# An attention and mixture-of-experts kernel: stack loads, statistics and narrow values in another order, and the last batch's scatters without landing waits

## The chip, the core and the metric

The kernel runs as one program on one core of a Trainium2 chip. Five engines work from their own instruction streams and wait for each other through semaphores: PE (TensorE, matrix products and transposes), DVE (VectorE), ACT (ScalarE), POOL (GpSimd) and SP (SyncE, which here only issues DMAs). The metric is the device time of one execution in microseconds, lower is better.

## What is computed

Two layers, each an attention block and a mixture of experts with the same expert weights, on x of 4 x 1024 x 256 in float32:

```python
x = x + attn_a(layernorm(x), ...)   # 16 heads of 16, causal, softmax with distance decay
x = x + ffn(layernorm(x), ...)
x = x + attn_b(layernorm(x), ...)   # 16 heads of 16, causal, plain softmax
x = x + ffn(layernorm(x), ...)

def ffn(x):                         # 4096 tokens
    shared = sum(relu(x @ w1 + b1) @ w2 + b2 for 2 shared experts) / 2
    probs = softmax(x @ router_w + router_b)       # 32 experts
    gates = top 6 of probs, divided by their sum
    routed = sum(gates[:, e] * (relu(x @ w1[e] + b1[e]) @ w2[e] + b2[e]) for 32 experts)
    return shared + routed
```

## The kernel before

Both layers run the same code, in four phases with a barrier of all five engines behind each (`phase_end`, L371). x lies in SBUF as 32 tiles of 128 tokens in four quarters of 8 tiles. A quarter is a batch, a block is half of one (512 tokens), so there are 8 blocks, numbered 0 to 7.

**Start of a layer.** DVE takes mean and variance of a quarter (`input_var`, L746, with ACT's square root, L1226), scales (`input_scales`) and normalises blocks (`normalise_block`, L733). In layer 1 it first adds the two expert sums into x: quarters 0 and 1 on DVE (L1209), 2 and 3 on POOL (L1506), all in the order of their loads. After the last layer the same adds stand before the result's stores.

**Phase 0, projections.** For each block TensorE forms q, k and v with split float32r products (L1541) and transposes v (L1551). DVE and POOL split q and k into a high and a low part (L782, L1414: POOL's `qk_lo`), DVE copies v into a staging tile `vst` with 32 columns a head: 16 values, then ones. SP stores q, k and v in HBM scratch (`store_block`, L412). Attention reads them back in units of four heads of one batch, 16 units. A unit's q and k lie in a stack, one of three slots. A slot is first zeroed (slot 0: half by DVE, L806, half by POOL, L1423, after all q and k work of block 5), then gets constant rows (`load_rows`, L434), then q and k (`load_stack`, L440), then, after a wait for the constant rows, two more rows (L443). The slots share their space with x's transposed blocks 0 to 3. Before the barrier TensorE and DVE compute unit 0's row maxima (L1576, L817). SP then waits for all stores (L472) and loads the negated maxima as a row of the stack (`load_neg_max`, L478), which the first scores need.

**Phase 1, attention.** Per unit 12 steps of scores (L1590), exponentials (ACT, L1282) and value products (L1607), with the next unit's maximum jobs and the routing of the batch before woven in. The value product's weights are 32 columns of `vreg`; a column of ones gives the softmax sum. Routing of a batch ends with `place_rows`, which computes the row index of each of a token's six copies. POOL's `dispatch(b)` (L1446) then scatters the batch's rows into per-expert lists: 48 indirect DMAs of 128 rows of 1280 B, six for each tile. They are counted on six semaphores, three for each half of the batch. In batches 0 and 1 POOL waits ahead of each third scatter for the three before, in batches 2 and 3 ahead of each for the one three places earlier. `dispatch(3)` falls into phase 2.

**Phase 2, shared experts.** TensorE computes them for the 8 blocks while batch 3 is routed; SP loads the remaining routed weights, the last of them (`load_w1(17, 32)`, L499) after the last shared sum is stored. The phase ends for SP when all scatters have landed.

**Phase 3, routed experts.** 128 tiles of 256 rows; POOL adds the results into the two sums (L1491).

On SP the weights for phases 2 and 3 that fit early are loaded at the end of phase 1: w1 of experts 10 to 16 in the last unit's turn, then the shared weights and w2 of 16 to 23 and 27 to 31, then the first two blocks of x for the shared experts.

## Time and profile before

| | |
|---|---|
| runs shown | 3131.27, 3128.80, 3125.81 us (median 3128.8) |
| the profiled execution | 3135.21 us, its span 3133.4 us |
| PE busy | 2614.6 us, 83% |
| DVE busy | 2075.2 us, 66% |
| ACT busy | 1643.9 us, 52% |
| POOL busy | 1395.5 us, 45% |
| DMA | 494.55 MB, mean 158 GB/s |
| mean granted clock of TensorE | 0.928 of 2.4 GHz |

The span runs from the first to the last instruction; the execution's own time is 1.8 us more. Busy shares are means over four kinds of phases that have different limits, so a change in one phase is read from that phase's rows: who is idle, until what. A timeline row gives start, duration, engine, line, operation, destination and source; in brackets stands the idle time before it and what ended it.

### The profile page before, as it was taken

Reading aid. Unit: us, or ns where it says so; the run is one execution under the profiler, and the core shown is the slowest. Engines: PE = TensorE matmul, PEld = TensorE weight load, DVE = VectorE, ACT = ScalarE, POOL = GpSimd, SP = SyncE. Lnnn points to the kernel's source line nnn. Section 1 sums busy time; section 2 is a strip of 40 time slices with the busy share of each in tenths; the row PEclk is TensorE's granted clock in tenths of the full one; section 3 lists DMA queues with packets and bytes.
Section 4 is the critical chain, followed back from the end, with each engine's and each line's share of the span. In section 5 each row is a group of like instructions: output and inputs, shape, how many; then the busy total and the mean of one; then the engine's idle time right before and its main releaser. Section 6 shows DMA issues by size and latency. Waiting matters only on the chain.

```text
span 3133.4 us, 72452 instructions
## 1 busy us (share of the span) xinstructions
PE 2614.6 (83%) x17832; PEld 1946.6 (62%) x17832; DVE 2075.2 (66%) x4624; ACT 1643.9 (52%) x2861; POOL 1395.5 (45%) x1046
## 2 busy tenths in 40 slices
PE   7699999999973799999385999999998728999992
PEld 5455565555553788888363555655555618888882
DVE  8666676776561687777395666766765517777872
ACT  3245444444411788888331554434444208888882
POOL 3430002314245688888544200023142457888885
PEclk9899999999987999999787999999999869999996
DMA  6975645555665789889859644564557648898988
GB/s 222 230 162 128 144 100 108 143 123 164 198 227 192 137 151 157 153 153 155 175 172 221 137 84 89 100 134 128 121 161 223 231 164 149 153 155 154 155 155 204
DMA packets 317281, 494.55 MB, mean 158 GB/s; under 512 B 55706, under 2 KB 225052, under 8 KB 311772
## 3 DMA queue, kind: packets, MB, share of 16 engines
q1 hardware_dynamic: 224908, 361.85, 43.9%
q0 software_dynamic: 92160, 130.08, 25.1%
q8 instruction: 106, 1.74, 0.2%
q14 instruction: 107, 0.88, 0.1%
HBM read 264.26 MB, written 256.77 MB: 166 GB/s over the span
## 4 chain that ended last, share of the span: by engine, by line
PE 45%; DMA 18%; issue 17%; POOL 6%; DVE 6%; SPq 3%; DVEq 2%; POOLq 1%; ACT 1%; ACTq 1%
PE ps L1576 10%; DMA expert_rows<-x 9%; PE ps L1590 9%; PE ps L1607 8%; DMA expert_sum<-x,route_u 5%; PE ps L1859 5%; PE ps L1877 4%; POOL expert_rows L1464 3%; PE ps L1594 2%; PE ps L1580 2%; SPq L424 2%; POOL expert_sum L1491 1%; DMA split<-rows_scratch 1%; DVE split L1171 1%; POOL split L1414 1%
## 5 line engine op out<-in xcount | busy, mean ns | idle before, releaser
L1282 ACT ACTIVATE work<-ps 128x1024 f32<-128x1024 f32 (+3 forms) x768 | 594.9, 810 | 679.0 <-PE ps L1594 458.1
L1464 POOL DMA_INDIRECT expert_rows<-x x372 | 365.4, 982 | 1272.1 <-DVE x L979 805.6
L1491 POOL DMA_INDIRECT expert_sum<-x,route_u x512 | 825.7, 1613 | 195.7 <-issue 92.5
L817 DVE TENSOR_REDUCE small<-ps 128x1 f32<-128x512 f32 (+3 forms) x1216 | 727.3, 656 | 216.9 <-PE ps L1580 145.1
L1576 PE MATMUL ps<-split 128*128 128x512 f32 (+3 forms) x1536 | 510.6, 408 | 72.3 <-DVE work L845 32.2
L1590 PE MATMUL ps<-split 128*128 128x512 f32 (+3 forms) x1536 | 501.6, 406 | 28.1 <-DMA split<-split 27.0
L1859 PE MATMUL ps<-split 128*88 128x256 f32 x3072 | 417.0, 285 | 86.2 <-DVE split L1171 50.4
L1859 PEld LDWEIGHTS ps<-split 128*88 128x88 f32 x3072 | 362.9, 155 | 134.9 <-issue 132.9
L1576 PEld LDWEIGHTS ps<-split 128*128 128x128 f32 x1536 | 275.0, 199 | 269.7 <-DVE small L817 144.8
L1877 PE MATMUL ps<-split 97*128 97x256 f32 x3072 | 408.8, 282 | 2.4 <-DVE split L1186 2.2
L1877 PEld LDWEIGHTS ps<-split 97*128 97x128 f32 x3072 | 384.7, 189 | 3.0 <-issue 2.9
L1590 PEld LDWEIGHTS ps<-split 128*128 128x128 f32 x1536 | 300.8, 202 | 86.7 <-ACT work L1282 40.8
L1607 PE MATMUL ps<-work,split 128*32 128x512 f32 (+3 forms) x3072 | 330.5, 505 | 2.8 <-ACT work L1282 2.8
L1346 ACT ACTIVATE x<-ps,osb 88x256 f32<-88x256 f32 x512 | 232.1, 471 | 30.8 <-issue 15.9
L1847 PE MATMUL ps<-ident,x 128*128 128x128 f32 x1024 | 156.7, 276 | 105.7 <-DMA osb<-in_b1r 105.7
L1360 ACT ACTIVATE split<-split 97x512 fp32r x256 | 161.4, 631 | 151.6 <-issue 138.3
L1594 PE MATMUL ps<-maskk,identb 128*128 128x128 bf16 x1024 | 234.6, 236 | 0.0
L1155 DVE CAST split<-work 128x352 fp32r x256 | 102.8, 402 | 188.7 <-issue 145.2
L1372 ACT ACTIVATE x<-ps,osb 128x256 f32<-128x256 f32 x512 | 212.1, 465 | 18.6 <-DMA expert_sum<-x,route_u 10.9
L1179 DVE TENSOR_TENSOR split<-split 97x512 fp32r<-97x512 f32 x256 | 176.3, 689 | 16.3 <-issue 7.4
L1847 PEld LDWEIGHTS ps<-ident,x 128*128 128x128 f32 x1024 | 120.3, 143 | 107.0 <-issue 107.0
L1580 PE MATMUL ps<-maskq,identb 128*128 128x128 bf16 (+2 forms) x704 | 185.7, 264 | 0.0
(179 smaller groups left out, 3152.2 us busy)
## 6 DMA issues: line engine op xcount, KB each, us to landing
x<-expert_rows SPq DMA_DIRECT2D x256, 320.0 KB
split<-qks_scratch SPq DMA_DIRECT2D x192, 256.0 KB
qks_scratch<-split SPq DMA_DIRECT2D x64, 512.0 KB, 4.5
expert_rows<-in_pads SPq DMA_DIRECT2D x65, 320.0 KB, 16.0
v_scratch<-work SPq DMA_DIRECT2D x64, 256.0 KB, 4.3
split<-v_scratch SPq DMA_DIRECT2D x32, 512.0 KB, 14.3
xT_scratch<-split SPq DMA_DIRECT2D x16, 1024.0 KB
split<-xT_scratch SPq DMA_DIRECT2D x16, 1024.0 KB
```

The costliest lines, as they stand in the source:

```text
L817: v.tensor_reduce(cols[:, heads[0]:heads[0] + len(heads), i], ps[:, task_bank(n), 0:w * len(heads)].rearrange("p (h k) -> p h k", k=w), AX ...
L1282: c.activation(pexp[:, (s % 2) * 2 + h, :, BLK - w:], ps[:, 2 * h:2 * h + 2, BLK - w:], ACT.Exp).then_inc(s_pe, 1)
L1464: pool.indirect_dma_start(rows, bass.IndirectOffsetOnAxis(ap=posu[b][:, t * 8 + k:t * 8 + k + 1], axis=0), row_tile(b, t // TPB, t % TPB), ...
L1491: pool.indirect_dma_start(acc[r], bass.IndirectOffsetOnAxis(ap=idx[:, j, k:k + 1], axis=0), ye[:, r3, k, :], None, compute_op=ALU.add).the ...
L1576: last = mm(bank[:, e, :], stack[:, r, 0, h, i * P:i * P + P], stack[:, r, 1, h, first:first + w], start=e == 0, stop=not diagonal and e = ...
L1580: last = mm(bank[:, :, w - P:w], identb[:, :], maskq[:, :].unsqueeze(1).broadcast_to([P, len(heads), P]), start=False, stop=True, skip_gro ...
L1590: last = mm(ps[:, h, BLK - w:], stack[:, r, 1, h, kb * P:kb * P + P], stack[:, r, 0, h, (qt + 1) * BLK - w:(qt + 1) * BLK], start=True, st ...
L1594: last = mm(ps[:, h, BLK - w:BLK - w + P], identb[:, :], maskk[:, :], start=False, stop=True, skip_group_check=True)
L1607: last = mm(ps[32 * h:32 * h + 32, 6, BLK - w:], vreg[:, r, kb, h, :], pexp[:, (s % 2) * 2 + h // 2, h % 2, BLK - w:], start=kb == 0, stop ...
L1847: last = tr(ps[:, r, k * TT + n * P:k * TT + n * P + P], xrow[:, r3, n, k * P:k * P + P], ident[:, :])
L1859: last = mm(ps[0:HC, 2 + c, 0:TT], w1e[:, r, ws, k * HID + c * HC:k * HID + c * HC + HC], xe[:, r, xp, k * TT:k * TT + TT], start=e == 0 a ...
L1877: last = mm(ps[:, 4 + 2 * (j % 2) + n, 0:D], he[0:HB, r, xp, c * TT + n * P:c * TT + n * P + P], w2e[0:HB, r3, ws, c * D:c * D + D], start ...
```

## The change

The change has five parts.

1. Values without padding: a head takes 17 columns (16 values, one column of ones) instead of 32, in `vst`, in the scratch and in `vreg`. The value product still reads 32 columns, at a step of 17, so that 15 of them belong to the next head and their results are not used. `vst` is laid out by unit, so that DVE copies four quarters of heads instead of two halves.
2. Slot 0 is zeroed by POOL alone, around block 4's low parts. Its constant rows are issued ahead of block 4's stores, its q and k ahead of block 5's. SP issues the stores of blocks 5, 6 and 7 in a row, then slot 1. The wait for all stores moves behind the load of the maxima row.
3. The early weights move forward: w1 of 10 to 16 into the turn of unit 13, the shared weights and w2 into that of unit 14.
4. The statistics, scales and first two normalised blocks of quarter 0 move to the end of the layer before, between DVE's two adds (`first_quarter`). For layer 0 they stand ahead of the loop, and they also run once after the last layer.
5. `dispatch(3)` has no waits between its scatters. The wait ahead of its first one stays. Batch 2 keeps its waits.

```diff
-    vds = nc.dram_tensor("v_scratch", (NU, P, NQB, HG * 32), F32, kind="Internal").ap()
+    vds = nc.dram_tensor("v_scratch", (NU, P, 2, TPB * HG * VW), F32, kind="Internal").ap()
...
-                with sp.Fori(0, B - 1) as b:
+                with sp.Fori(0, B - 2) as b:
                     for r in range(2):
                         store_block(b, r)
...
                 load_rows(0)
                 for r in range(2):
                     sp.wait_ge(s_pd[r], (L * B + 1) * 64 + 64)
+                store_block(B - 2, 0)
                 load_stack(0, 0)
-                store_block(B - 1, 0)
+                store_block(B - 2, 1)
+                for r in range(2):
+                    store_block(B - 1, r)
                 load_rows(1)
                 load_stack(1, 1)
-                store_block(B - 1, 1)
                 phase_end(sp, L, 0)
...
-                for r in range(2):
-                    sp.wait_ge(s_pd[r], (L * B + B) * 64 + 64)
-                    sp.wait_ge(s_vd[r], (L * B + B) * 64 + 64)
...
                 load_neg_max(0)
+                for r in range(2):
+                    sp.wait_ge(s_pd[r], (L * B + B) * 64 + 64)
+                    sp.wait_ge(s_vd[r], (L * B + B) * 64 + 64)
                 load_values(0, 0)
...
                 for u in range(NU):
+                    if u == NU - 2:
+                        sp.wait_ge(s_pv, (L * NU + NU - 3) * NS + NS + 2)
+                        if L == 0:
+                            sp.wait_ge(s_init, 128)
+                        apart(sp)
+                        sp.dma_start(raw.rearrange("p r n -> p (r n)"), wsd).then_inc(s_raw, 16)
+                        load_w2(16, 24)
+                        load_w2(27, 32)
...
-                    if u == NU - 1:
+                    if u == NU - 3:
                         sp.wait_ge(s_mr, TASKS + route_task(B - 2, 3) + 1 + 3)
                         apart(sp)
                         load_w1(EARLY, 17)
-                sp.wait_ge(s_pv, (L * NU + NU - 3) * NS + NS + 2)
-                apart(sp)
-                sp.dma_start(raw.rearrange("p r n -> p (r n)"), wsd).then_inc(s_raw, 16)
                 sp.dma_start(b1, a["b1"]).then_inc(s_shared, 16)
-                load_w2(16, 24)
-                load_w2(27, 32)
...
+            def first_quarter(N):
+                input_var(N, 0)
+                input_scales(N, 0)
+                for r in range(2):
+                    normalise_block(N, r, r)
...
-                    for f in range(2):
-                        last = v.tensor_copy(vst[:, r, :, 8 * f:8 * f + 8, 0:HD],
-                                             ps[:, 6 + f, :].rearrange("p (t h c) -> p t h c", t=TPB, h=8))
+                    for u in range(HG):
+                        last = v.tensor_copy(vst[:, r, u, :, :, 0:HD],
+                                             ps[:, 6 + u // 2, :].rearrange("p (t h c) -> p t h c", t=TPB, h=8)
+                                             [:, :, u % 2 * HG:u % 2 * HG + HG, :])
...
-                dve.wait_ge(s_pj, (L * NBLK + 4) * 6)
-                v.memset(stack32[64:P, 0, 0], 0.0).then_inc(s_zq, 1)
...
                     v.tensor_tensor(xq, xq, summ[:, q], ALU.add).then_inc(s_ca[q], 1)
+                    if q == 0:
+                        first_quarter(L + 1)
...
-                with pool.Fori(0, B - 1) as b:
+                with pool.Fori(0, B - 2) as b:
                     for r in range(2):
                         qk_lo(b, r)
                 pool.wait_ge(s_pj, (L * NBLK + 4) * 6)
-                pool.wait_ge(s_pl, (L * NBLK + 6) * 4 + 4)
-                apart(pool)
-                p.memset(stack32[64:P, 0, 1], 0.0).then_inc(s_zero[0], 1)
-                pool.wait_ge(s_zero[0], L + 1)
+                for r in range(2):
+                    pool.wait_ge(s_pl, (L * NBLK + 4 + r) * 4 + 4)
+                    apart(pool)
+                    p.memset(stack32[64:P, 0, r], 0.0).then_inc(s_zero[0], 1)
+                    pool.wait_ge(s_zero[0], L * 2 + r + 1)
+                    apart(pool)
+                    qk_lo(B - 2, r)
...
-                            if n >= AHEAD and b >= B - 2:
+                            if n >= AHEAD and b == B - 2:
...
-                            elif n >= AHEAD and n % AHEAD == 0:
+                            elif n >= AHEAD and n % AHEAD == 0 and b < B - 2:
...
-                        last = mm(ps[32 * h:32 * h + 32, 6, BLK - w:], vreg[:, r, kb, h, :],
+                        at = (kb * HG + h) * VW
+                        last = mm(ps[32 * h:32 * h + 32, 6, BLK - w:], vreg[:, r, at:at + 32],
```

Three places where instructions move. First the SP queue at the end of phase 0; its destinations and sources are `split<-rows_scratch` for constant rows, `split<-qks_scratch` for q and k, `split<-split` for the maxima row. Before, from the end of the loop over blocks 0 to 5 on:

```order
L434 DMA split<-rows_scratch 20x4x1024 [waits first_query_stack_zeroed,stack_zeroed0,constant_rows_stored]
L440 DMA split<-qks_scratch 16x4x1024 [waits qk_stored1,qk_stored0]
L440 DMA split<-qks_scratch 16x4x1024 x5
L443 DMA split<-rows_scratch 2x4x1024 [waits constant_rows_loaded0]
L418 DMA qks_scratch<-split 128x2x512 [waits qk_lo_done]
L424 DMA v_scratch<-work 128x4x128 [waits v_staged]
L434 DMA split<-rows_scratch 20x4x1024 [waits stack_zeroed1]
L440 DMA split<-qks_scratch 16x4x1024 x6
L443 DMA split<-rows_scratch 2x4x1024 [waits constant_rows_loaded1]
L478 DMA split<-split 1x32x128 [waits phase_done,v_stored1,qk_stored1,task_done,v_stored0,qk_stored0]
```

And now, from the end of the loop over blocks 0 to 3 on:

```order
L434 DMA split<-rows_scratch 20x4x1024 [waits stack_zeroed0,constant_rows_stored]
L420 DMA qks_scratch<-split 128x2x512 [waits qk_lo_done,qk_stored0,qk_stored1]
L426 DMA v_scratch<-work 128x272 [waits v_staged]
L440 DMA split<-qks_scratch 16x4x1024 x6
L443 DMA split<-rows_scratch 2x4x1024 [waits constant_rows_loaded0]
L420 DMA qks_scratch<-split 128x2x512 [waits qk_lo_done]
L434 DMA split<-rows_scratch 20x4x1024 [waits stack_zeroed1]
L440 DMA split<-qks_scratch 16x4x1024 x6
L443 DMA split<-rows_scratch 2x4x1024 [waits constant_rows_loaded1]
L477 DMA split<-split 1x32x128 [waits phase_done,task_done]
```

Slot 0 has moved ahead of two blocks' stores, slot 1 behind the last one, and the maxima row no longer waits for stores.

Then POOL from its last wait for row indices on, which is `dispatch(3)`. Before, its head, of which the last two rows stand for 45 such waits:

```order
L1450 REGISTER_ALU [waits row_indices_ready]
L1464 DMA expert_rows<-x 140288x320 [waits rows_dispatched12,rows_dispatched10,rows_dispatched11]
L1464 DMA expert_rows<-x 140288x320 x2
L1457 ISA
L1464 DMA expert_rows<-x 140288x320 [waits rows_dispatched00]
L1464 DMA expert_rows<-x 140288x320 [waits rows_dispatched01]
```

And now, to its end:

```order
L1462 REGISTER_ALU [waits row_indices_ready]
L1476 DMA expert_rows<-x 140288x320 [waits rows_dispatched12,rows_dispatched10,rows_dispatched11]
L1476 DMA expert_rows<-x 140288x320 x41
L1476 DMA expert_rows<-work,x 140288x320 x6
L377 REGISTER_ALU
```

47 of the 48 scatters now stand in a row; 45 had a wait of their own.

Last, DVE at the end of a layer. Before, behind the barrier of phase 3:

```order
L1207 REGISTER_ALU [waits phase_done]
L1209 TENSOR_TENSOR x<-x,split 128x2048 [waits sums_loaded0]
L1209 TENSOR_TENSOR x<-x,split 128x2048 [waits sums_loaded1]
L698 REGISTER_ALU
L698 COMPARE_AND_BRANCH
```

And now, with the steps of the variance left out:

```order
L1215 TENSOR_TENSOR x<-x,split 128x2048 [waits sums_loaded0]
L733 REGISTER_ALU [waits x_loaded0]
L687 BN_STATS small<-x 128x6 [waits sums_added0]
L687 BN_STATS small<-x 128x6 x7
L727 TENSOR_SCALAR work<-x,osb 128x256 [waits dve_chain,xT_psum_ready]
L1215 TENSOR_TENSOR x<-x,split 128x2048 [waits sums_loaded1]
L760 REGISTER_ALU
L760 COMPARE_AND_BRANCH
```

The statistics and the normalising of two blocks stand between the two adds, ahead of the loop's branch.

## Rows read from the trace of the kernel before

**Rows 1.** Timeline of the SP queue: start, duration, instruction, count [idle before, by whom ended].
```profile
100.02 1.45 SPq L434 DMA_DIRECT2D split<-rows_scratch  x2
...
127.49 2.14 SPq L434 DMA_DIRECT2D split<-rows_scratch  x2
...
140.85 0.24 SPq L443 DMA_DIRECT2D split<-rows_scratch  x1
...
159.18 1.22 SPq L478 DMA_DIRECT2D split<-split  x2
```

**Rows 2.** Timeline of PE, 62 to 168 us.
```profile
124.29 1.11 PE L1576 MATMUL ps<-split 128*128 128x128 f32 x4 [14.00 <-DMA split<-rows_scratch]
...
162.09 0.79 PE L1590 MATMUL ps<-split 128*128 128x512 f32 x1 [13.52 <-DMA split<-split]
```

**Rows 3.** Windows, phase 0: stretch, length, busy by engine, PEclk, DMA share, GB/s.
```profile
84.00:102.00 18.00, 17.15 (x87) 14.06 (x87) 15.12 (x16) 8.26 (x12) 13.64 (x9) 1.00 1.01 338
105.00:117.00 12.00, 4.43 (x23) 3.30 (x21) 3.08 (x4) 2.14 (x4) 10.86 (x5) 0.77 1.04 117
153.00:157.00 4.00, 0.00 (x0) 0.00 (x0) 0.00 (x0) 1.28 (x1) 0.84 (x1) 0.50 0.83 262
```

**Rows 4.** Timeline of POOL, phase 0: block 4's low parts, slot 0's memset.
```profile
76.47 5.95 POOL L1414 TENSOR_TENSOR split<-work,split 128x512 fp32r<-128x512 f32 x4 [5.03 <-DVE split L782]
...
90.98 3.52 POOL L1423 MEMSET split<- 64x4096 f32 x1 [0.16 <-POOL split L1414]
```

**Rows 5.** Timeline of POOL, scatters of batches 2 and 3, layer 0.
```profile
830.81 0.96 POOL L1464 DMA_INDIRECT expert_rows<-x  x1 [41.66 <-DVE x L979]
...
840.37 0.96 POOL L1464 DMA_INDIRECT expert_rows<-x  x1 [4.84 <-DMA expert_rows<-x]
...
933.10 0.96 POOL L1464 DMA_INDIRECT expert_rows<-x  x1 [8.57 <-DMA expert_rows<-x]
...
1010.48 0.96 POOL L1464 DMA_INDIRECT expert_rows<-work,x  x1 [0.30 <-DMA expert_rows<-work,x]
1011.75 0.96 POOL L1464 DMA_INDIRECT expert_rows<-work,x  x1 [0.31 <-issue]
```

**Rows 6.** Windows, the ends of phase 2 in layers 0 and 1.
```profile
990.00:999.00 9.00, 0.00 (x0) 0.00 (x0) 0.00 (x0) 0.00 (x0) 2.88 (x3) 0.50 1.05 388
...
2548.00:2568.00 20.00, 0.00 (x0) 0.00 (x0) 0.00 (x0) 0.00 (x0) 15.12 (x17) 0.50 0.34 123
```

**Rows 7.** Timeline of the SP queue, layer 0: the last routed weights.
```profile
988.44 0.71 SPq L499 DMA_DIRECT2D work<-in_w1r  x1
```

**Rows 8.** Timeline of PE, layer 0: the first tile's transposes.
```profile
1026.11 1.09 PE L1847 MATMUL ps<-ident,x 128*128 128x128 f32 x4 [44.23 <-DMA osb<-in_b1r]
```

**Rows 9.** Timeline of POOL, layer 1: first and last scatter of batch 3.
```profile
2490.36 0.97 POOL L1464 DMA_INDIRECT expert_rows<-x  x1 [2.41 <-DMA expert_rows<-x]
...
2570.32 0.97 POOL L1464 DMA_INDIRECT expert_rows<-work,x  x1 [0.30 <-issue]
```

**Rows 10.** Timeline of DVE, layer 0: batch 3's rows are placed.
```profile
914.60 0.15 DVE L979 COPY work<-x 128x1 f32<-128x1 f32 x1
```

**Rows 11.** Timelines of DVE at the start of layer 0 and of layer 1.
```profile
8.96 2.71 DVE L684 BATCH_NORM_STATS2 small<-x 128x6 f32<-128x256 f32 x8 [0.18 <-issue]
...
16.86 0.95 DVE L764 CAST split<-work 128x1536 fp32r<-128x1536 f32 x1
...
1548.89 2.29 DVE L1209 TENSOR_TENSOR x<-x,split 128x2048 f32<-128x2048 f32 x1 [29.87 <-DMA split<-expert_sum]
...
1564.42 2.71 DVE L684 BATCH_NORM_STATS2 small<-x 128x6 f32<-128x256 f32 x8 [4.35 <-issue]
...
1577.33 0.95 DVE L764 CAST split<-work 128x1536 fp32r<-128x1536 f32 x1
```

**Rows 12.** Timeline of DVE at the kernel's end.
```profile
3104.26 2.29 DVE L1209 TENSOR_TENSOR x<-x,split 128x2048 f32<-128x2048 f32 x1 [28.62 <-DMA split<-expert_sum]
```

**Rows 13.** Line L1607, its weight loads: duration ns min/median/max, first and last start.
```profile
L1607 PEld LDWEIGHTS ps<-work,split x3072: 106/109/156, 170.5 to 2400.3; 128*32 128x32 f32 x192
```

More of the change, by code:

```diff
@@ L674, in _ @@
             dve.sem_inc(s_thl, 2)
-            chain = [0]
+            chain, layer = [0], [0]
             def link(ins):
@@ L686, in statistics, with linked, row_var @@
                 return last
+            def linked():
+                dve.wait_ge(s_chain, layer[0] * CHAIN + chain[0])
+            def row_var(st, sv):
+                me, ve, mo, vo = (st[:, :, s] for s in (1, 2, 4, 5))
+                v.tensor_tensor(sv[:, 0], me, mo, ALU.subtract)
+                v.tensor_tensor(sv[:, 1], me, mo, ALU.add)
+                link(v.tensor_tensor(sv[:, 2], ve, vo, ALU.add))
+                linked()
+                v.tensor_tensor(sv[:, 3], sv[:, 0], sv[:, 0], ALU.mult)
+                link(v.tensor_scalar(sv[:, 4], sv[:, 2], 1.0 / D, EPS, ALU.mult, ALU.add))
+                linked()
+                v.scalar_tensor_tensor(sv[:, 5], sv[:, 3], 0.25, sv[:, 4], ALU.mult, ALU.add).then_inc(s_var, 1)
@@ new lines, in normalise_block, with input_var @@
+            def normalise_block(N, blk, r):
+                dve.wait_ge(s_tp, N * NBLK + blk + 1)
+                for j in range(TPB):
+                    t = blk * TPB + j
+                    last = v.tensor_scalar(xn[:, r, j, :], x[:, ds(t * D, D)], sv[:, 8, ds(t, 1)],
+                                           sv[:, 9, ds(t, 1)], ALU.mult, ALU.add)
+                last.then_inc(s_xn, 1)
+            def input_var(N, q):
+                dve.wait_ge(s_x[q], 16)
+                dve.wait_ge(s_ca[q], N + 1)
+                apart(dve)
+                link(statistics(8 * q, 8))
+                linked()
+                row_var(stat[:, 8 * q:8 * q + 8, :], sv[:, :, 8 * q:8 * q + 8])
```

111 lines of the change are left out of this document (41 added, 70 removed).

## The prediction

> **What bounds the kernel now.** I read the page's shares and its chain of waits first: TensorE is the busiest engine and carries most of the chain, DMA comes next. TensorE's part lies in attention and in the tile loop, which the change leaves alone. The DMA part lies in three gaps where TensorE is idle, once per layer or between layers, and there the stage timelines decide.
>
> Gap one is the end of phase 0. TensorE has no work for 14.00 us until the first stack has landed at 124.29, and again 13.52 us until the row of negated maxima arrives at 162.09 [rows 2]. The SP queue issues the constant rows for slot 0 at 100.02, those of slot 1 at 127.49, and the maxima row only at 159.18 [rows 1]. DMA is saturated there: share 1.01 at 338 GB/s over 84 to 102, and also 1.04 at only 117 GB/s while rows and stacks are written [rows 3]. So the gap is a queue of bytes, and an order within it.
>
> Gap two is the end of phase 2. The last 96 scatters (batches 2 and 3) run on POOL from 830.81 to 1012.71; batch 3 alone from 933.10, 48 scatters in 79.6 us [rows 5]. TensorE idles 44.23 us until the first tile's transpose at 1026.11, 13.4 us after POOL's last issue [rows 8]. The last weights were issued at 988.44 [rows 7]. In layer 1 batch 3 takes from 2490.36 to 2571.29, 80.9 us [rows 9].
>
> Gap three is between the layers: the first quarter is summed by 1551.18, but its statistics start at 1564.42 [rows 11].
>
> **The end of phase 0, with thinner v stores.** Sizes are from the shapes. A block stores q and k with 4 x 512 KB, 2.1 MB, and v with 4 x 256 KB, 1.05 MB. At 338 GB/s the first takes 6.2 us; the v stores alone run at 262 GB/s [rows 3], 4.0 us. The new v is 17 of 32 columns, 0.56 MB; in pieces of 1088 B instead of 512 B I take the 338 GB/s, 1.6 us. A block falls from 10.2 to 7.8 us. Rows plus stack of one slot are 0.66 + 1.57 = 2.2 MB at 117 GB/s, 19 us (5.6 and 13.4).
>
> As a check, the old kernel from 84 on has four blocks and two slots, 41 + 38 = 79 us, so it would end at 163; its maxima row left at 159.18, so the model is 4 us too long. Now the new order. POOL finishes block 4's subtractions at 82.42 [rows 4]; one memset (3.52 us, as the one at 90.98 [rows 4]) stands before that, the second behind it, so the rows of slot 0 are issued at 86, not 100. Then rows 5.6, block 4 7.8, stack 13.4: slot 0 lands at 113 instead of 124.3. The maximum jobs take 24.3 us (from 124.29 to where TensorE goes idle, 13.52 us ahead of 162.09 [rows 2]) and then end at 137. But behind the stack wait three block stores (23 us) and slot 1 (19 us), the DMA ends at 86 + 31 + 38 = 155, less the 4 us of the check 151. The maxima row leaves when SP is through its last row wait, and is then behind slot 1's stack in the queue: first scores at about 153 instead of 162.09. **Gain 9 us a layer, 18 together.** Bounds: 5, if the v stores stay at 262 GB/s and nothing else overlaps; 16, if a small DMA isn't held up by the stack, since then only SP's wait counts (rows of slot 1 issued at 131, 11 us to land as from 127.49 to 140.85 [rows 1], then 2.9 us as now).
>
> That a small load waits here shows in the 2-partition load behind slot 0's stack: its landing ends TensorE's 14.00 us, long after its issue. The Trainium skill, "DMA: Bandwidth & Descriptors", section "Queues, rings and completion order", says that on each DMA engine descriptors are consumed in ring order; by that rule the 16 us bound is out and 9 stands, without it the sum would be 14 us larger. It speaks against the full worth of the reordering, since SP now issues more ahead of the maxima row.
>
> **The scatters.** Without waits POOL issues one each 1.27 us (1010.48 to 1011.75 [rows 5]; the many other unheld neighbours read alike), so 48 take 47 x 1.267 + 0.96 = 60.5 us. Against 79.6 and 80.9 us that takes off 19.1 and 20.4. The DMA can take that: over 2548 to 2568, with scatters alone at about this pace, the share is 0.34 [rows 6]. The wait ahead of batch 3 for batch 2's second half stays. Batch 2 gains too: its first and fourth scatter are 9.56 us apart [rows 5], at free pace 3.8. The transfers that crowd them are the shared weights, the w2 parts and w1 (4.9 MB), which now go out one to two units earlier. So batch 3 starts 5.8 earlier; at least 0, at most 18, as its rows are placed at 914.75 [rows 10].
>
> Next in line in layer 0 is w1: 2.7 MB issued at 988.44, DMA full over 990 to 999 at 388 GB/s [rows 6, 7], landed about 1001, with the first tile's rows right behind. So the first transpose comes near 1004 instead of 1026.11: 22 us, though POOL is done 24.9 earlier. In layer 1 w1 has landed before 2548, since DMA then moves scatters alone [rows 6], 23 us before POOL ends, so POOL's 5.8 + 20.4 = 26.2 us count nearly in full. **Gain 48.** Bounds: 39.5 - 3 without batch 2's part and with stores slowed by the denser scatters; 61 with batch 3 starting at its earliest in layer 1 and layer 0 held at 23.
>
> **The moved loads.** Raw shared weights, w2 and w1, 4.9 MB at 338 GB/s, are 15 us at the border of units 13 and 14. They pass the maxima row of unit 15 on SP, which is due two thirds into a unit of 42 us ((830.81 - 162.09) / 16). Cost 0; if that cover were gone, up to 15 us a layer. The scatters of batch 1 are queued beside them, but their successor starts at 830.81 after 41.66 us of idle POOL [rows 5].
>
> **Between the layers.** The first quarter's statistics to normalised rows take 7.9 us undisturbed (8.96 to 16.86 at the kernel's start [rows 11]). From 1551.2 they end at 1559.1, the second add (2.29) at 1561.4; the 4.35 us behind it that the row at 1564.42 shows make it 1565.8, where the weight split can start; before, it started at 1577.33 [rows 11]. That is 11.5 us, of which POOL's two adds may eat what they now cost DVE: 1564.42 to 1577.33 is 12.9 us for the 7.9. **Gain 7**, bounds 4 and 11. At the very end the same block sits before the second add: the first ends at 3106.55 [rows 12], then 7.9 and 2.29 give 3116.7, 4 us later than the second add's end now. The stores leave in order, and the last one waits for POOL's second add (L1506), which nothing moves: **cost 1**, bounds 0 and 5.
>
> **Small edits at 0**: the v memset shrinks 16 times, DVE loses one memset at slot 0, the v copies become four halves instead of two; TensorE is the busier engine there. Together -2 to +2 us.
>
> Sum: 18 + 48 + 7 - 1 = 72. The profiled execution, 3135.2 us (span 3133.4), would become 3063. The median of the runs, 3128.8, is 6.4 lower; from it, 3057.
>
> **Rivals.**
> 1. The maxima row isn't held up by slot 1's stack: 16 a layer instead of 9, 3043. For it: the stacks are written by many short transfers in parallel. Against: the 14.00 us above. 20%.
> 2. The scatter queue fills and holds POOL instead of the semaphores. POOL waited up to 8.57 us for a landing [rows 5], six or seven scatters' worth at free pace; what the queue holds beyond three shows nowhere. Then only batch 2's part is left of the 48, some 12: 3093. Against: the share of 0.34. 12%.
> 3. Slower: the weights of the value products are now 32 columns at a step of 17, 68 B, so they start unaligned and overlap. TensorE loads them 3072 times, in 0.109 us each (median [rows 13]). If a load grew by 23 ns and nothing hid it, all 72 us were gone; at twice 0.109 with half hidden it is +167 - 72 = +95, 3224. Against: each load can run under the product of the head before, and moves as many bytes as now. 3%.
> 4. The new order does nothing, since slot 0 is still late, and the layer start is eaten by POOL: only the scatters' 48, 3081. 8%.
>
> **How the numbers follow.** Forecast 57%: 3057. Its own bounds: gains of 10 + 36 + 4 - 5 - 2 = 43 to 32 + 61 + 11 + 2 = 106, so 3086 to 3023; both ends need every bound at once. 3028 to 3088 holds most of the forecast, rivals 1 and 4: about 82%. A measurement can tell 0.2%, 6 us. Faster 0.96, same 0.01, slower 0.03.
>
> **What would show it.** Right: slot 0's rows issued near 86, maximum jobs from about 113, first scores near 153; batch 3's scatters 1.27 us apart with no landing waits; first tile transposes 22 and 26 us nearer to the start of batch 2; weight split 7 us or more sooner after 1551.2. Wrong: scatters of batch 3 with gaps or long issues, w1 landing later than 1001, value-weight loads above 0.109 us, or a wait for the maxima row in units 14 and 15.

## The result, and the profile after

The changed kernel is slower: 3218.4 us in the median of 4 runs (3193.6 to 3223.9), against 3127.7 (3125.8 to 3131.3) for the kernel before on the same chip. The ratio is 1.0273, with a 95% interval of 1.0217 to 1.0329. Forecast were 3057 us, with 3028 to 3088 as the range; the result lies 161 us above it, and on the other side of the kernel before. The profiled run took 3213.5 us, its span is 3211.7 at a mean clock of 0.916 (before: 3133.4 at 0.928), so 78.3 us are to be found in the trace.

First where they are. Each boundary of a stage has a row that stands right behind it. Of the kernel after, from SyncE's timeline (start us, us, engine and line, operation, out<-in): the load of the first unit's maxima, which opens phase 1, the table's load, which opens phase 2, and the first tile's rows, which open phase 3, for both layers:

```profile
150.22 1.23 SPq L477 DMA_DIRECT2D split<-split  x2
887.01 0.33 SPq L581 DMA_DIRECT2D work<-in_table  x1
1062.87 0.36 SPq L641 DMA_DIRECT2D x<-expert_rows  x1
...
1746.85 1.25 SPq L477 DMA_DIRECT2D split<-split  x2
2477.53 0.33 SPq L581 DMA_DIRECT2D work<-in_table  x1
2654.70 0.37 SPq L641 DMA_DIRECT2D x<-expert_rows  x1
```

The same of the kernel before (its first is in [rows 1]):

```profile
842.06 0.33 SPq L578 DMA_DIRECT2D work<-in_table  x1
1022.98 0.38 SPq L638 DMA_DIRECT2D x<-expert_rows  x1
...
1719.26 1.25 SPq L478 DMA_DIRECT2D split<-split  x2
2403.15 0.33 SPq L578 DMA_DIRECT2D work<-in_table  x1
2581.49 0.37 SPq L638 DMA_DIRECT2D x<-expert_rows  x1
```

And VectorE's timeline of after, at the first sum of each layer (before: [rows 11] and [rows 12]); the statistics of the next layer's first quarter now follow it:

```profile
1593.49 2.29 DVE L1215 TENSOR_TENSOR x<-x,split 128x2048 f32<-128x2048 f32 x1 [30.81 <-DMA split<-expert_sum]
...
3182.60 2.29 DVE L1215 TENSOR_TENSOR x<-x,split 128x2048 f32<-128x2048 f32 x1 [29.02 <-DMA split<-expert_sum]
3185.04 2.71 DVE L687 BATCH_NORM_STATS2 small<-x 128x6 f32<-128x256 f32 x8
```

The differences between these rows give the ledger:

| stretch, us | before | after | change |
|---|---|---|---|
| start to maxima of unit 0, layer 0 | 159.2 | 150.2 | -9.0 |
| phase 1, layer 0 | 682.9 | 736.8 | +53.9 |
| phase 2, layer 0 | 180.9 | 175.9 | -5.1 |
| phase 3, layer 0 | 525.9 | 530.6 | +4.7 |
| first sum to maxima of unit 0, layer 1 | 170.4 | 153.4 | -17.0 |
| phase 1, layer 1 | 683.9 | 730.7 | +46.8 |
| phase 2, layer 1 | 178.3 | 177.2 | -1.2 |
| phase 3, layer 1 | 522.8 | 527.9 | +5.1 |
| first final sum to the end | 29.1 | 29.1 | 0.0 |

100.7 of the loss are in phase 1, of which the forecast said nothing at all, and phase 2 has not given the 48 that it was to give.

Now the place in phase 1. Its last 45 us are nearly empty. The windows of after, 845 to 870 us (columns as in [rows 3]: busy time and instruction count of TensorE, of its weight loads, of VectorE, ScalarE and POOL, then the granted clock, the DMA engines' share, GB/s):

```profile
845.00:870.00 25.00, 0.00 (x0) 0.00 (x0) 0.00 (x0) 0.00 (x0) 18.90 (x21) 0.50 0.35 127
```

Three engines stand still, and the DMA engines are a third busy. Only POOL works, and SyncE issues nothing between 804.83 and 887.01. What each engine did there, from the timelines of PE, ScalarE, VectorE and POOL in turn (in brackets the idle time before, and what ended it):

```profile
842.52 0.66 PE L1620 MATMUL ps<-work,split 128*32 128x128 f32 x8 [6.36 <-ACT work L1290]
875.13 1.11 PE L1630 MATMUL ps<-ident,osb 128*128 128x128 f32 x4 [31.95 <-ACT osb L1278]
```

```profile
842.09 0.38 ACT L1290 ACTIVATE work<-ps 128x256 f32<-128x256 f32 x1 [3.84 <-remote]
874.40 0.60 ACT L1278 ACTIVATE osb<-ps 128x512 f32<-128x512 f32 x1 [31.93 <-remote]
```

```profile
885.53 0.26 DVE L848 RECIPROCAL small<-ps 128x16 f32<-128x16 f32 x1 [59.47 <-remote]
885.82 0.42 DVE L851 TENSOR_TENSOR work<-ps,small 128x256 f32<-128x256 f32 x1
```

```profile
822.12 0.96 POOL L1476 DMA_INDIRECT expert_rows<-x  x1 [32.92 <-issue]
...
843.03 0.96 POOL L1476 DMA_INDIRECT expert_rows<-x  x1 [0.30 <-DMA expert_rows<-x]
...
882.28 0.96 POOL L1476 DMA_INDIRECT expert_rows<-x  x1 [0.31 <-issue]
```

The last value products of unit 15 end at 843.18 (842.52 and 0.66). ScalarE's copy at L1278 (`evacuate`) waits for nothing but `s_pv`, which counts the value products, and `s_mj`, which counts TensorE's transposes and other small jobs. Both are raised by TensorE alone. Yet it starts at 874.40, 31 us after the products. TensorE's transposes at L1630 follow it within 0.13 us (875.00 to 875.13), so ScalarE's signal came at once. They end at 876.24; VectorE, which waits for them alone, starts at 885.53, 9.3 us late.
Meanwhile POOL issues batch 2's 48 scatters in 60.2 us from the first to the last, one every 1.27, where the kernel before took 92.8. Its waits for landings are still in the code and hardly hold it: its idle time between two of them is 0.30 us, and at most 0.69. Nothing else moves then, and the scatters land in time. That is the second half of the finding. The moved loads (a w2 stretch, the raw weights, w1) used to fill the DMA engines at just this time; the windows 815 to 820 us, of before and then of after:

```profile
815.00:820.00 5.00, 5.00 (x31) 2.21 (x31) 0.55 (x3) 2.53 (x5) 0.00 (x0) 0.70 1.03 370
```

```profile
815.00:820.00 5.00, 4.68 (x33) 2.13 (x34) 3.50 (x16) 3.87 (x5) 0.00 (x0) 1.00 0.00 0
```

The DMA share goes from 1.03 to 0.00, and batch 2's row forms in the gap.

Phase 2 repeats it with batch 3, whose waits the change did remove. POOL's first and last scatter and TensorE's timeline of after:

```profile
954.58 1.20 POOL L1476 DMA_INDIRECT expert_rows<-x  x1 [71.34 <-DVE work L985]
...
1015.56 0.96 POOL L1476 DMA_INDIRECT expert_rows<-work,x  x1 [0.30 <-issue]
```

```profile
1023.17 1.09 PE L1805 MATMUL ps<-ident,work 128*128 128x128 f32 x4 [28.28 <-DVE work L1110]
...
1054.71 0.63 PE L1805 MATMUL ps<-ident,work 128*128 128x128 f32 x4 [0.87 <-DVE work L1110]
1071.44 2.00 PE L1860 MATMUL ps<-ident,x 128*128 128x128 f32 x8 [16.11 <-DMA osb<-in_b1r]
```

The 48 take 61.9 us to the end of the last, against 60.5 forecast. But they start at 954.58, where the forecast had 927: their rows are placed later, since phase 1 ends 45 us later. And phase 2's products, which ended at 981.9 in the kernel before (1026.11 less the 44.23 of waiting in [rows 8]), now end at 1055.3: the engines end phase 2, and no longer the scatters.

### The profile page after: what moved, and what is told of

Read it like the earlier page. It is cut to its first block, busy times and chain, and to the rows that moved or that the text cites. A ratio compares the mean times of both kernels' runs of the same rounds, so it can differ in the third digit from the quotient of the medians.

```text
span 3211.7 us, 72334 instructions
## 1 busy us (share of the span) xinstructions
PE 2636.3 (82%) x17832; PEld 1961.2 (61%) x17832; DVE 2082.4 (65%) x4682; ACT 1646.2 (51%) x2863; POOL 1402.4 (44%) x1048
## 4 chain that ended last, share of the span: by engine, by line
PE 47%; issue 13%; DVE 12%; DMA 12%; another core or an unknown queue 5%; POOL 3%; DVEq 2%; ACT 2%; SPq 1%; POOLq 1%; PEldq 1%; ACTq 1%; PEld 0%
PE ps L1588 10%; PE ps L1602 10%; PE ps L1620 8%; DMA expert_sum<-x,route_u 6%; PE ps L1872 4%; PE ps L1890 3%; DMA expert_rows<-x 2%; PE ps L1606 2%; PE ps L1592 2%; POOL expert_sum L1503 2%; PE ps L1665 2%; DVE split L1177 2%; PE ps L1782 1%; PE ps L1793 1%
## 5 line engine op out<-in xcount | busy, mean ns | idle before, releaser
L1588 PE MATMUL ps<-split 128*128 128x512 f32 (+3 forms) x1536 | 512.4, 409 | 65.2 <-DVE work L851 34.5
L1185 DVE TENSOR_TENSOR split<-split 97x512 fp32r<-97x512 f32 x256 | 176.2, 688 | 15.9 <-issue 8.2
L1192 DVE TENSOR_TENSOR split<-x,split 88x512 fp32r<-88x512 f32 x256 | 174.1, 680 | 13.4 <-ACT split L1359 11.7
(178 smaller groups left out, 3143.1 us busy)
```

The costliest lines, as they stand in the source:

```text
L1588: last = mm(bank[:, e, :], stack[:, r, 0, h, i * P:i * P + P], stack[:, r, 1, h, first:first + w], start=e == 0, stop=not diagonal and e = ...
```

## The experiments

All times are medians, all ratios against the kernel before on the same chip. The experiments ran on four chips, where the kernel before took 3123.9 to 3127.2 us, so differences of a few us between them mean little. **Theory A**: a long row of scatters without a pause, one every 1.27 us, makes TensorE's signals late; batch 2's row exists because of the moved loads, batch 3's because of the removed waits. **Theory B**: only the scatters without waits do harm. **Theory C**: the loads in their new place collide with the attention units. **Theory D**: it is a matter of how many scatters and bytes are under way, whatever their spacing.

### One part undone, and one part alone

`undo_issue`, the fifth part undone:

```
-                            if n >= AHEAD and b == B - 2:
+                            if n >= AHEAD and b >= B - 2:
...
-                            elif n >= AHEAD and n % AHEAD == 0 and b < B - 2:
+                            elif n >= AHEAD and n % AHEAD == 0:
```

> The changed kernel with the fifth part undone: batch 3's scatters wait for landings again. Theory A (a long row of scatters every 1.27 us makes TensorE's signals late; batch 2's row comes from the moved loads, which left the DMA engines idle from 806 to 830): the end of phase 1 still loses about 45 us a layer, because batch 2's scatters do not change (822 to 882, 60 us for 48); batch 3's may keep a pitch of 1.27 too where nothing else moves, and so the time stays above 3180, 3190 to 3230. Theory B (only the unthrottled scatters of batch 3 do harm): the loss goes, and the time is that of before less the gains of the border and of phase 0, 3085 to 3110. Theory C (the early loads collide with the attention units' own): still slow, 3200 to 3220, but with batch 2's scatters slower than 60 us.

3098.8 us (3091.3 to 3109.1), ratio 0.9909 (0.9879 to 0.9939). This is theory B's number, and theory A's lowest, 3180, was 81 us too high. The trace shows why, in ScalarE's and SyncE's timelines of this run:

```profile
830.73 0.60 ACT L1278 ACTIVATE osb<-ps 128x512 f32<-128x512 f32 x1 [4.73 <-remote]
```

```profile
833.65 0.33 SPq L581 DMA_DIRECT2D work<-in_table  x1
```

The same copy waits for the same late signal, 4.7 us instead of 31.9. Phase 1 has then ended by 833.65, SyncE's loads of phase 2 start, the scatters have to wait for landings again, and the row ends at twelve. A reading that fits is that a row is a trap that holds itself: late signals keep SyncE from issuing, and an idle DMA system keeps the row unbroken. Batch 2's code is the same in both kernels, and here it began at 817.1, in after at 822.1. Why the trap closes in the changed kernel and not here is not shown: five runs of this one lie between 3091 and 3109, four of that one between 3194 and 3224, so it isn't chance from run to run. The moved loads alone are thus not enough for the row.

`undo_loads`, the third part undone (the diff's hunks on w1, the raw weights and w2 taken back):

> The changed kernel with the third part undone: w1, the raw shared weights and w2 are loaded at the end of phase 1 again. Theory A: batch 2's scatters are held back by those loads as before (about 93 us for 48, none over 10 in a row), the 32 us wait of ScalarE for a matmul's signal at the end of phase 1 goes, about 90 us are regained; batch 3's 48 in a row still make TensorE's signals late in phase 2, so that of the 48 us forecast little is left: 3090 to 3130. Theory B: no change, 3210 to 3225, since the loss is put down to batch 3. Theory C: 3060 to 3130.

3129.9 us (3119.4 to 3143.1), 1.0014 (0.9993 to 1.0034). Theory A fits, theory B falls: 89 us come back although batch 3's scatters stay without waits. Their row still costs; TensorE's timeline in this run:

```profile
985.18 2.93 PE L1792 MATMUL ps<-split 128*128 128x512 f32 x6 [32.49 <-ACT work L1321]
```

`loads_alone`, the kernel before with the third part only:

> The kernel before with the third part alone. Theory A: batch 2's scatters run in one row of 60 us, the end of phase 1 loses 40 to 50 us a layer, 3190 to 3225. Theory B: the forecast's price for the moved loads, nothing, 3120 to 3135. Theory C: 3190 to 3225 too, but with the loss in units 13 to 15 (760 to 810), ahead of batch 2's scatters.

3142.6 us in the median of ten runs, but these spread from 3113.4 to 3207.7. The ratio, 1.002 (0.998 to 1.006), is of the seven shortest; the medians of all give 1.005. Theory A's range, from 3190 up, holds one run of the ten, and no theory named a spread. It is what the trap would make, closed in one layer, in both or in none, but the profiled run took 3120.3 and has no long row in batch 2. The runs that would show it were not profiled, so the trap is not shown here; this run shows only that the cost is not constant.

`issue_alone`, the kernel before with the fifth part only:

> The kernel before with the fifth part alone. The forecast's step: 44 to 48 us faster, 3080 to 3085. Theory A: batch 3's 48 scatters stand in one row of 61 us, in which TensorE's signals come late and phase 2's last blocks stand still, so most of the gain is lost again: 3110 to 3140. Theory B: slower than before by 40 us a layer, 3190 to 3220.

3154.3 us (3152.5 to 3160.2), 1.0082 (1.0055 to 1.0109): slower by 28, where the forecast's step says 48 faster, and 14 above theory A's range, 36 under theory B's. TensorE's timeline has one long wait in batch 3's row:

```profile
999.23 1.22 PE L1780 MATMUL ps<-split 128*128 128x512 f32 x2 [38.37 <-ACT work L1314]
```

### The length of a row

If a pause is what lets the signals through, the rows can be cut. These four start from the changed kernel, whose loads stay moved. Rows of k wait, at every k-th scatter of batches 2 and 3, for the landing of the ones before; `rows3`, `rows6` and `rows12` have k = 3, 6 and 12:

```
-                            if n >= AHEAD and b == B - 2:
-                                r, m = divmod(n - AHEAD, TPB * TOPK)
-                                pool.wait_ge(s_disp[r][m % AHEAD], ...)
-                                apart(pool)
-                            elif n >= AHEAD and n % AHEAD == 0 and b < B - 2:
+                            if n >= AHEAD and n % (AHEAD if b < B - 2 else k) == 0:
```

> The changed kernel with batches 2 and 3 issued three at a time, each three after the landing of the three before, as batches 0 and 1 are. Theory A (TensorE's signals come late in proportion to the length of a row of scatters without a pause): no row over 3, no wait of ScalarE on TensorE's signals over 5 us at the end of phase 1 or in phase 2; batches 2 and 3 take 90 to 110 us each, so that the scatters again end the layer: 3085 to 3125. Theory D (a jam by the count of scatters or their bytes, wherever the pauses are): 3150 to 3220.

> As that with rows of six in batches 2 and 3. Theory A: about 75 to 80 us a batch (48 scatters of 1.27 us and seven waits for a landing of 2.3 us), signals late by 2 us at most, 3060 to 3095, faster than rows of three. Theory D: 3150 to 3220.

> As that with rows of twelve. Theory A: some 70 us a batch, signals late by up to about 5 us near a row's end (4.3 us after nine scatters in the run without the fifth part), 3055 to 3110; with rows as short as this the jam of 32 us does not come. Theory D: 3150 to 3220.

`rows3` took 3188.8 us (3182.2 to 3200.1), 1.0206 (1.0168 to 1.0245). `rows6` took 3096.4 (3095.8 to 3102.9), 0.9909 (0.9879 to 0.9940), and `rows12` 3094.1 (3081.1 to 3107.6), 0.9891 (0.9844 to 0.9939). By the time alone `rows3` speaks for theory D (3150 to 3220), the other two against it. TensorE's waits (us in total, times, longest; 780 to 1080 us) speak against it in all three. `rows3`:

```profile
PE ps L1856 <- DMA osb<-in_b1r: 100.8, 2, 98.7
...
PE ps L1626 <- ACT osb L1278: 1.8, 1, 1.8
```

`rows6`:

```profile
PE ps L1856 <- DMA osb<-in_b1r: 51.2, 2, 49.0
...
PE ps L1801 <- DVE work L1110: 2.8, 2, 1.9
```

`rows12`:

```profile
PE ps L1856 <- DMA osb<-in_b1r: 15.9, 1, 15.9
...
PE ps L1801 <- DVE work L1110: 10.8, 3, 5.0
PE ps L1616 <- ACT work L1290: 6.9, 1, 6.9
```

In rows of three no signal is late by more than 2 us, and TensorE waits 98.7 us at the start of phase 3 for scatters that are simply too slow: 123.2 us for batch 2 and 93.9 for batch 3. Theory A's price for `rows3`, 3085 to 3125, took the pace from batches 0 and 1 too kindly. In rows of six 49.0 of that wait are left, in rows of twelve 15.9. These 15.9 are no longer due to the scatters: the changed kernel has 16.1 there, though its row ended 39 us before TensorE's last products of phase 2. Meanwhile the late signals grow to 5.0 and 6.9. The two costs trade, and the best row is in between or a mixture.

`pause` keeps the change's waits and puts POOL work between any two scatters:

```
+        idle = sb("idle", [P, 384], F32)
...
+                            if b >= B - 2:
+                                p.memset(idle[:, 0:384], 0.0)
+                                pool.drain()
                             pool.indirect_dma_start(
```

> The changed kernel with its waits as they are and a short piece of POOL work, a memset of 128 x 384 and a drain, ahead of every scatter of batches 2 and 3, so that no two stand 1.27 us apart. Theory A in its strict form (the pitch of 1.27 us is what makes the signals late, and any pause between scatters lets them through): no wait over 5 us, and the time goes by the pitch that comes out, 3090 to 3160 at 1.8 to 2.2 us. If only the landing of all issued scatters clears it, the signals stay late in the long rows of batch 3, and the time is 3180 to 3230.

3460.3 us (3458.1 to 3462.8), 1.107 (1.104 to 1.110). The pause came out far longer than meant, 3.3 us from scatter to scatter and more in batch 2, so the time is above every forecast. It does say that without dense issue no signal is late: TensorE's longest wait on VectorE's copies at L1111, which hang on them, is 1.8 us, and of TensorE's 86 updates beside batch 2 in layer 0 none is over 0.04 us late. (Batch 3 tests nothing here: TensorE is done with phase 2 before it starts.) But at 3.3 us from one to the next nearly every scatter has landed before the next is issued, so it does not tell the dense issue from the missing landings. Batch 2's row in the changed kernel does: its waits allow three scatters under way at most, and the signals are as late there as in batch 3, which has none.

`b2_rows12` changes batch 2 alone, to rows of twelve; batch 3 stays without waits:

```
+                            if n >= AHEAD and b < B - 1 and n % (AHEAD if b < B - 2 else 12) == 0:
```

> The changed kernel with one edit: batch 2's scatters in rows of twelve instead of one wait per scatter; batch 3's stay without waits, and the loads stay moved. Theory A (the price of the moved loads is batch 2's unbroken row and nothing else): the 32 us wait at the end of phase 1 goes in both layers and 80 to 90 us with it, down to the run without the third part, 3115 to 3140; the wait of about 30 us in batch 3's row of 48 stays. If the loads' place itself costs, 3180 to 3220.

3141.4 us (3121.8 to 3152.2), 1.0045 (1.0017 to 1.0072): 77 of the changed kernel's us come back, with the loads in their new place. This rules theory C out. TensorE's longest wait is now in phase 2, in batch 3's row:

```profile
PE ps L1789 <- ACT work L1322: 37.8, 1, 37.8
```

`mix_6_12` has rows of six in batch 2 and rows of twelve in batch 3:

```
+                            if n >= AHEAD and n % {B - 2: 6, B - 1: 12}.get(b, AHEAD) == 0:
```

> Batch 2 in rows of six and batch 3 in rows of twelve. In rows of six phase 2's products are done at 961 and phase 3 waits for the scatters until 1006; in rows of twelve the products are done at 998, with the scatters at 989. Theory A: batch 2 ends at 912 and batch 3 starts at 915 as in rows of six, takes 68 us as in rows of twelve and ends at 983, the products by 985: phase 3 about 10 us a layer earlier than either, 3070 to 3085. If batch 3's rows of twelve alone hold the products up: 3090 to 3100, no gain.

**3071.0 us** (3067.2 to 3082.2), 0.9833 (0.9787 to 0.9879), faster than both kernels: 53 us under before, 1.7%, with all five parts of the change in place but for the form of the waits. Its waits of TensorE:

```profile
PE ps L1856 <- DMA osb<-in_b1r: 28.2, 2, 25.9
...
PE ps L1801 <- DVE work L1110: 5.2, 4, 2.1
...
PE ps L1789 <- ACT work L1322: 4.2, 1, 4.2
```

`mix_6_24`, the same with 24 for 12, asks for the size in between:

> Batch 2 in rows of six and batch 3 in two rows of twenty-four. Theory A, now asked for the size: batch 3 takes 64 us instead of 70 and would end phase 2 by 5 us a layer earlier, but in a row of 24 (30 us) a signal of TensorE can be late by 10 to 20 us where one of twelve made it 5: 3080 to 3115, slower than 3071. If lateness is not a matter of the row's length but of rows without any end (48): 3055 to 3075.

3121.3 us (3096.7 to 3133.8), 0.9976 (0.9951 to 1.0002): 50 us slower than with twelve, a little beyond the range. The waits:

```profile
PE ps L1801 <- DVE work L1110: 19.4, 3, 18.1
...
PE ps L1789 <- ACT work L1322: 14.2, 3, 10.3
PE ps L1778 <- ACT work L1311: 6.5, 1, 6.5
```

So the longest wait behind a signal of TensorE in batch 3, layer 0, was 1.9 us in rows of six, 4.2 and 5.0 in rows of twelve (`mix_6_12`, `rows12`), 18.1 in rows of twenty-four, and 28 to 38 in the four runs with a row of forty-eight. In layer 1 it was 13 us with twenty-four and 9 to 35 with forty-eight, so the size varies from place to place. The recorded updates show the same without the detour over waits. How late at least TensorE's latest one was behind the end of its matmul, from the first scatter of a batch to 8 us behind the last, over both layers:

| scatters in a row | batches | latest update of TensorE, us |
|---|---|---|
| 1 | `pause`, batch 2 | 0.04 to 0.19 |
| 3 | `rows3`, batch 2 | 1.0 to 1.3 |
| 6 | `rows6`, both; `mix_6_12` and `mix_6_24`, batch 2 | 1.1 to 3.2 |
| 12 | `rows12`, both; `b2_rows12`, batch 2; `mix_6_12`, batch 3 | 4.4 to 7.3 |
| 24 | `mix_6_24`, batch 3 | 18.9 to 19.1 |
| 48 | after, both; `undo_loads`, `issue_alone`, `b2_rows12`, batch 3 | 13.6 to 46.8 |

In all of these stretches no update of VectorE or ScalarE was more than 0.02 us behind. (Only semaphores that one engine alone raises are counted.) Theory A's form, late in proportion to the row, holds roughly; a wait per scatter that lets a long row form is no better than none.

### The other parts, and the loads again

`parts124` is the changed kernel without its third and fifth parts, `border` the kernel before with the fourth alone:

> The changed kernel without its third and fifth parts: v's compact copy, slot 0's early zeroing and stack, and the statistics between the layers. By the forecast's terms 18 for phase 0 and 7 for the border less 1: 24 under before, 3100 to 3105. By the first trace, whose phases 0 are 4.0 and 11.9 us shorter and whose phases 3 are 4.4 and 5.0 longer: 3115 to 3120.

> The kernel before with the fourth part alone, the first quarter's statistics between VectorE's two last sums. By the forecast's terms 6 faster (7 at the border, 1 lost at the end): 3119 to 3122. If what is moved only lengthens phase 3's end by what it saves in phase 0: 3125 to 3128.

`parts124` took 3101.2 us (3092.4 to 3112.4), 0.9930 (0.9904 to 0.9955), and `border` 3113.1 (3105.5 to 3120.8), 0.9963 (0.9945 to 0.9981). The forecast's 3100 to 3105 for the first holds. The second gained 11 where 6 were forecast, and the first two parts together are left with 12 or less (10 by the ratios) instead of 18.

`mix_loads_back` takes the third part out of `mix_6_12`, and `rows_alone` is the kernel before with nothing but the rows of six and twelve:

> The run with rows of six and twelve, with the third part undone. It asks what the moved loads are worth once no long row can form. The forecast's term is nothing: 3065 to 3080. If the loads at the end of phase 1 hold batch 2's scatters back (92 us for 48 in the run without the third part, 86 to 90 with it) and meet phase 2's own loads: 3075 to 3095.

> The kernel before with nothing but batch 2's scatters in rows of six and batch 3's in rows of twelve. Theory A: of the scatters' 48 us the part that rows of twelve allow, batch 3 in 70 instead of 79 us and no long row: 10 to 15 us a layer, 3095 to 3110. If the gain needs the moved loads: 3115 to 3130.

`mix_loads_back` took 3100.0 us (3093.5 to 3107.9), 0.9898 (0.9868 to 0.9927), `rows_alone` 3115.3 (3106.5 to 3124.8), 0.9945 (0.9919 to 0.9972). The first is beyond both of its ranges, the second in the one for a gain that needs the moved loads. With the rows cut, the moved loads are worth 29 us by the medians, 20 by the ratios: batch 2's scatters take 86 to 90 us instead of 101, and batch 3 starts that much earlier. Neither half has the gain by itself. Over `parts124`, whose scatters wait as before, the cut rows bring 1 us without the moved loads (3101.2 to 3100.0), and the moved loads bring 2 without the cut rows (3098.8, `undo_issue`); both together bring 30. By the ratios these are 10, 7 and 30, so the two single gains lie within the noise, and the surplus of the pair is 13 to 27.

The changed kernel's own two steps, in one table:

| with the first, second and fourth parts, us | loads as before | loads moved |
|---|---|---|
| a wait per scatter | 3101.2 | 3098.8 |
| batch 3 without waits | 3129.9 | 3218.4 |
| rows of six and twelve | 3100.0 | 3071.0 |

## Why the prediction was wrong, step by step

- **Phase 0, 9 us a layer: its mechanism failed, and that the ledger has 9.0 in layer 0 is in part luck.** By the runs the first two parts are worth 10 to 12 for both layers, not 18. Slot 0's constant rows are issued at 88.55, where 86 was forecast. But the max jobs did not start at 113: they start at 124.84, before at 124.29 [rows 2], now held by VectorE's copies of v for the last block. (The bound of 16 also reads 11 us between two rows that are 13.4 apart; with that it is 15.) What was saved lies behind them: the stores stand ahead of the second stack, and their landings are waited for only after the maxima's load. First scores start at 155.42, not at 153; before, 162.09 [rows 2].
- **Between the layers, 7 us, less 1 at the end: right, and low if anything.** Border and phase 0 of layer 1 together were to give 16, and the ledger has 17.0; alone the part gave 11 over both. The end of the kernel costs nothing in the ledger: 29.1 us from the first final sum, before and after.
- **Compact v and its unaligned weights: right.** The value products took 508 ns each, before 505, their weight loads 0.109 us in the median, as before. The rival that put the slower outcome there, 3224 at 3%, hit the number and had the wrong mechanism. Its number is no support for it.
- **Moved loads, 0: the first step that failed.** Alone among the terms it was priced by what the loads themselves need. The prediction asked what hides them. It even saw that they had crowded batch 2's scatters, and booked the relief as a gain of 5.8 us. They were the traffic that made these scatters pause. With them gone and batch 3 without waits, the row of 48 formed, in both layers, and phase 1 became 53.9 and 46.8 us longer. With a wait per scatter in both batches the 0 was right, as a size (3101.2 to 3098.8); beside batch 3 without waits it is 89 us (3129.9 to 3218.4), and next to cut rows the same move is worth 20 to 29 in favour. So the sum failed as a sum too: it added two terms that depend on each other. Why batch 3's waits decide over batch 2's row is open.
- **Scatters without waits, 48: the second that failed.** Pace and length came as forecast, 61.9 us for 48 against 60.5. That the engines' own work in phase 2 would keep its pace beside them was taken for granted, and that step is false: the row makes TensorE wait 28 to 38 us in one place, and the step that was to gain 48 costs 28 by itself (29 beside the first, second and fourth parts).
- **The sign was to be had from the trace of before.** It has late signals too, though small. A row of before's TensorE timeline and two of its VectorE, in a stretch where batch 3's scatters come in rows of eight and nine:

```profile
969.34 0.63 PE L1792 MATMUL ps<-ident,work 128*128 128x128 f32 x4 [3.05 <-issue]
```

```profile
968.50 0.69 DVE L1104 COPY work<-ps 128x512 f32<-128x512 f32 x1 [4.37 <-remote]
972.79 0.69 DVE L1104 COPY work<-ps 128x512 f32<-128x512 f32 x1 [3.60 <-remote]
```

  The transposes end at 969.97, and VectorE's copy, which waits for them, starts at 972.79, 2.8 us late, on a release that no instruction explains. The copy before it had waited 4.37 us in the same way. The prediction read that stretch for when the scatters end [rows 5, 6], not for what the other engines do beside them. It also put 12% on a rival in which the dense issue holds POOL; the same row held the other engines instead, which no rival had.
- **Phase 3, not mentioned, +4.7 and +5.1.** The first transposes start 8.6 us after the first tile's load (1062.87 to 1071.44), before 3.1 us (1022.98 to 1026.11). The last stretch of w1 is issued at 1059.51, right ahead of the first rows, where before it had 34.5 us of lead [rows 7]. Phase 2 ended with the engines and not with the scatters, and the order of loads was made for the opposite. No run tested this alone.

## What to carry to other kernels

Before a wait is taken away or traffic moved, ask what it was slowing down, and whether that can do harm at full speed: the waits and the loads here were brakes on the scatters. Where POOL issues many indirect DMAs beside work of TensorE, issue them in short rows with a wait for the landings between them, and find the length by trial; six and twelve were best here, three starved the next phase and twenty-four stalled TensorE. When two edits each do little alone, run the four combinations: these two are worth next to nothing apart from each other (2 and 1 us by the medians), 30 together, and with no waits in place of short rows minus 117.

## What the runs showed of the hardware

In a long row of indirect DMAs from POOL, one every 1.27 us, semaphore updates by TensorE arrive late: by the waits behind them 28 to 38 us at the worst in rows of 48, up to 18 in rows of 24, 7 in rows of 12 and 2 in rows of 6; by the recorded updates 14 to 47, 19, 4 to 7 and 1 to 3, and 0.04 to 0.19 where some 3.3 us and more lie between two scatters. Those of ScalarE and VectorE come within 0.02 us in the same stretches, and their operations keep their length (0.69 us for a copy of 128x512 at 975.38, in batch 3's row, 0.68 at 950.08, before it). The DMA engines are 0.35 busy, and TensorE's products keep their pace where it has its inputs (1.52 us for six in the row, 1.53 behind it). The lateness ends soon after the row: the last late signal of phase 1 comes at 885.5, 3.2 us behind the start of the last scatter, and batch 3's last three come together, from 1022.31 to 1022.46, 6.9 us behind. What TensorE's signals share with POOL's issue is not shown, nor whether the results come late with them; that it is the issue and not the bytes rests on the DMA share and on batch 2's row, with three under way at most; scatters of fewer bytes were not tried.

The Trainium skill, on its page "TensorE: Matmul & The Clock Gate", section "The cost: per-tile semaphore tail", gives some 26 ns for each increment. Away from the scatters the trace agrees in order, with no update over 0.05 us behind its matmul from 886 to 954 us; beside them it has the updates up to 31 us behind in the changed kernel, over 1,000 times that figure, and the measurement decides. The Trainium skill, on its page "SBUF — State Buffer", section "SBUF: two separate sides", says that a compute operation cannot be slowed by a DMA. The trace agrees for the operations, by the lengths above. It does not follow that the engines aren't held up: through the late signals three of them stood still for 30 us beside a DMA system at a third of its load.
